# Moving the transposes of q and k to the head of a slot in an attention and GRU kernel

## The chip, the cores and the metric

The kernel runs on one core of one Trainium2 chip. The metric is the device time of one execution in microseconds (us). Before the change it is 2216.08 us, the median of 3 runs (2215.71 to 2216.1).

## The reference, cut to what matters

Two layers with residual connections work on x of shape (4, 512, 512), all in fp32. The first is attention with 16 heads of 32 columns; the second is a GRU that walks over the 512 positions one after the other.

```
# layer 0
xn  = rms_norm(x, g_norm) * (1 + scale) + shift        # scale, shift from emb @ W_emb + b_emb
q, k, v = heads(xn @ W_qkv)                            # 16 heads of 32
q, k = rms_norm(q, g_q), rms_norm(k, g_k)
attn = softmax(q @ k.T * 32 ** -0.5)
o = attn @ v
x = x + o + o @ W_out
# layer 1: GRU over 512 steps
r = sigmoid(x_t @ W_ir + h @ W_hr + b);  z = sigmoid(...)
n = tanh(x_t @ W_in + b + r * (h @ W_hn + b))
h = (1 - z) * n + z * h;   x_t = x_t + h
```

## The kernel before, in words

Each engine (TensorE is called PE, VectorE DVE, ScalarE ACT, GpSimd POOL) has its own program, written out by hand, and runs it strictly in its order; semaphores tie the programs together. The attention takes the first 556 us or so, the GRU the rest.

Attention is cut into units of one group of four heads by 128 positions. There are 4 batches x 4 groups x 4 blocks of 128 = 64 units, and every engine walks over `N_SLOTS` = 71 slots. One slot of PE works on several units at different stages (lines 395 to 474): it projects unit `n = slot` to q, k and v (`project`, line 403), transposes the normalised q and k of unit `i = slot - 2` (`transpose_qk`, line 361), forms the scores of unit `m = slot - 6`, transposes that unit's softmax weights (line 464), multiplies the transposed weights of unit `m - 1` with v (line 443), and transposes the reciprocal row sums of `m - 1` (`transpose_rexp`, line 398). In this document the last is the "rexp transpose", and the product with v is "the values". A slot's order on PE is: rexp transpose, four score matmuls (one head each, on four row groups of the array; an fp32 matmul is two instructions in the trace), the two transposes of q and k, values (on four column groups), first projection quarter, transposes of the probabilities of heads 0 and 1, second quarter, those of heads 2 and 3, third and fourth quarter.

At the end of a slot there may be a piece (`piece_of`, lines 147 to 157, and `run_piece`, line 378): four transposes of raw x ("x" piece), four transposes of scaled x ("xn" piece), or a block of eight matmuls of the output projection ("y" piece). There are 12 of each kind in the 64 slots. Each piece writes all of PSUM bank 7, `PM`. It is evicted in the next slot: an x piece by ACT (line 602), an xn piece by DVE (line 737) where its chunk is even and by ACT (line 594) where it is odd, a y piece by DVE (line 743).

The transposes of q and k write the same bank. So `transpose_qk` waits for three things (lines 361 to 370): that ACT has evicted the previous unit's q and k (`qkT_ready`), that the piece of the slot before has been evicted (`await_piece`), and that DVE has written the normalised q and k (`qn_done`, line 753). In slots 0 to 5 it is called at the end of the slot (line 471); that call is not part of the change. From slot 6 on, for units 4 to 63, it is called from line 432.

The softmax runs beside it: DVE takes the maximum of each head's scores (line 774), ACT exponentiates (line 648), PE transposes the result, DVE (line 778, heads 0 and 1) and ACT (line 653, heads 2 and 3) evict it. ACT's order in a slot is: v and the squares of the unit projected before (lines 616, 619), the eviction of an x or odd xn piece, the reciprocals (line 641), q and k (line 632), four exponentials, two evictions. DVE's is: sum of squares (line 759), the eviction of a y or even xn piece, four maxima, two evictions, reciprocal, normalised q and k, the copy that feeds the rexp transpose (line 788).

Of the kernel before, what the change touches and what calls it, by code (L numbers as in the profile page):

```python
# [46 lines left out]
LAG = 6  # L47
ALL_TILES = B * N_TILES
# [13 lines left out]
def attention_gru_kernel(nc, x, cond, W_emb, b_emb, g_norm, W_qkv, g_q, g_k, W_out,  # L62
                         W_ih, W_hh, b_ih, b_hh, out):
    with ExitStack() as ctx:
# [82 lines left out]
        def piece_of(slot):  # L147
            b, u = divmod(slot, N_TILES)
            if not 0 <= slot < ALL_TILES:
                return None  # L150
            if b >= 1 and X_SLOT <= u < X_SLOT + KT:
                return "x", b, u - X_SLOT
            if b >= 1 and Y_SLOT <= u < Y_SLOT + KT:
                return "y", b - 1, u - Y_SLOT
            if b < B - 1 and XN_SLOT <= u < XN_SLOT + KT:
                return "xn", b + 1, u - XN_SLOT
            return None
# [160 lines left out]
        def _(pe):  # L318
            def transpose(dst, src):
                return nc.tensor.transpose(dst, src, ident[:])  # L320
# [27 lines left out]
            def await_piece(slot):  # L348
                piece = piece_of(slot)
                if piece is not None:  # L350
                    kind, b, c = piece
                    if kind == "x":
                        pe.wait_ge(s["xT_ready"], b * KT + c + 1)
                    elif kind == "y":
                        pe.wait_ge(s["x1_ready"], b * KT + c + 1)
                    elif c % 2 == 0:
                        pe.wait_ge(s["xnT_dve"], 2 * b + c // 2 + 1)
                    else:
                        pe.wait_ge(s["xnT_act"], 2 * b + c // 2 + 1)

            def transpose_qk(i):
                if i == 0:
                    pe.wait_ge(s["xT_ready"], KT)
                else:
                    pe.wait_ge(s["qkT_ready"], i)
                await_piece(i + 1)
                pe.wait_ge(s["qn_done"], i + 1)
                for a in range(2):
                    last = transpose(ps[:, PM, P * a:P * a + P], qn[:, i % 2, P * a:P * a + P])
                last.then_inc(s["tqk_done"], 1)  # L370
# [7 lines left out]
            def run_piece(slot):  # L378
                kind, b, c = piece_of(slot)
                pe.wait_ge(s["qkT_ready"], slot - 1)  # L380
                if kind == "x":
                    for t in range(TT):
                        last = transpose(ps[:, PM, P * t:P * t + P], xb[:, t, P * c:P * c + P])
                    last.then_inc(s["x_ps"], 1)
                elif kind == "xn":
                    pe.wait_ge(s["xr_ready"], b * TT + TT)
                    for t in range(TT):
                        last = transpose(ps[:, PM, P * t:P * t + P], xr[:, t, P * c:P * c + P])
                    last.then_inc(s["xn_ps"], 1)
                else:  # L390
                    pe.wait_ge(ld_wout, 16)
                    pe.wait_ge(s["oT_ready"], b * G + G + 1)
                    out_projection(c, PM)

            for slot in range(N_SLOTS):
                n, i, m = slot, slot - 2, slot - LAG

                def transpose_rexp():

                    pe.wait_ge(s["rexp_done"], m)  # L400
                    transpose(ps[:, PJ[slot % 2], 3 * P:4 * P], rexp[:]).then_inc(s["rtr_done"], 1)

                def project(k):
                    b, tile = divmod(n, N_TILES)
                    g, t = divmod(tile, TT)
                    return nc.tensor.matmul(ps[:, pj(n), 0:3 * P], xnT[:, b % 2, k, P * t:P * t + P],  # L406
                                            wqkv[:, k, :].rearrange("p (a g n) -> p a g n", a=3, g=G)[:, :, g, :],
                                            start=(k == 0), stop=(k == KT - 1))

                if 0 <= m - 1 and (i < ALL_TILES or m == ALL_QUADS):  # L410
                    transpose_rexp()
                if 0 <= m < ALL_QUADS:

                    g, q = divmod(m, TT)
                    if q == 0:
                        pe.wait_ge(s["qkT_ready"], TT * g + TT)
                    for hh in range(4):

                        if m == 0:
                            pass  # L420
                        elif hh < 2:
                            pe.wait_ge(s["ptev_dve"], 2 * m - 1 + hh)
                        else:
                            pe.wait_ge(s["ptev_act"], 2 * m - 3 + hh)

                        head = slice(DH * hh, DH * hh + DH)
                        nc.tensor.matmul(ps[:, SC[hh], :], qkT[head, g % 2, 0, P * q:P * q + P], qkT[head, g % 2, 1, :],  # L427
                                         start=True, stop=True, tile_position=(DH * hh, 0)).then_inc(s["s_done"], 1)
                        if hh == 0 and i >= ALL_TILES:
                            transpose_rexp()  # L430

                if slot >= LAG and i < ALL_TILES:
                    transpose_qk(i)
                if 0 <= m - 1 < ALL_QUADS:

                    g, q = divmod(m - 1, TT)
                    if q == 0:
                        pe.wait_ge(s["oT_ready"], g + 1)
                    pe.wait_ge(s["ptev_dve"], 2 * m)
                    pe.wait_ge(s["ptev_act"], 2 * m)  # L440
                    for kc in range(TT):
                        for hh in range(4):
                            last = nc.tensor.matmul(  # L443
                                ps[QD * hh:QD * hh + QD, PO, P * q:P * q + P],
                                v_sb[:, g % G, kc, QD * hh:QD * hh + QD], probsT[:, hh, kc, :],
                                start=(kc == 0), stop=(kc == TT - 1), tile_position=(0, QD * hh))
                    last.then_inc(s["pv_done"], 1)

                if n < ALL_TILES:
                    if n % N_TILES == 0:  # L450
                        pe.wait_ge(s["xnT_dve"], 2 * (n // N_TILES) + 2)
                        pe.wait_ge(s["xnT_act"], 2 * (n // N_TILES) + 2)
                    if n >= 6:
                        pe.wait_ge(s["qn_done"], n - 1)
                    elif n >= 4:
                        pe.wait_ge(s["xT_ready"], KT)
                    if 0 <= m - 1:
                        pe.wait_ge(s["r_ready"], m)
                    project(0)
                for hh in range(4):  # L460
                    if 0 <= m < ALL_QUADS:
                        pe.wait_ge(s["exp_done"], 4 * m + hh + 1)
                        for kc in range(TT):
                            last = transpose(ps[:, SC[hh], P * kc:P * kc + P], probs[:, hh, P * kc:P * kc + P])
                        last.then_inc(s["pt_done"], 1)
                    if n < ALL_TILES and hh == 1:
                        project(1)
                if n < ALL_TILES:
                    project(2)
                    project(3).then_inc(s["proj_done"], 1)  # L470
                if slot < LAG and 0 <= i:
                    transpose_qk(i)
                if piece_of(slot) is not None:
                    run_piece(slot)
# [56 lines left out]
            for step in range(T):  # L531
# [14 lines left out]
                if n < N_BLK and q < 6 * B and step + LEAD >= 12:  # L546
                    b, i = divmod(q, 6)
# [371 lines left out]
```

## Time and profile before

| | us |
|---|---|
| median of 3 runs | 2216.08 |
| the profiled execution's own time | 2220.15 |
| its span, first to last instruction | 2218.3 |
| PE busy | 2141.1 |
| DVE busy | 1239.9 |
| ACT busy | 1150.6 |
| POOL busy | 204.8 |
| granted TensorE clock, mean | 0.999 |

The times of the table's engines are sums over the whole span. PE's matmul records overlap each other by a little, since matmuls are pipelined and their ends are modelled; the distance from one start to the next says more than a record's length. In a timeline, consecutive instructions of one kind are one row: the second number is from the first start to the last end. The number in square brackets is idle time of the engine just before the row, with what ended it; "issue" there means that the profile names no releaser. "PEld" is the loading of weights, which runs beside the matmuls.

### The profile page before, as it was taken

To read this page: it belongs to the slowest core of one execution; us is meant where nothing else is said; L and a number is where in the kernel's file an instruction comes from. 1 tells how busy PE (TensorE), PEld (TensorE's weight loads), DVE (VectorE), ACT (ScalarE), POOL (GpSimd) and SP (SyncE) were. 2 spreads that over 40 slices of the span, in tenths; PEclk is the share of its full clock that TensorE was granted. 3 is DMA by queue.
4 is the path that set the end of the run, shared out by engine and by line. 5 is a ranking of instruction groups with operands and counts; after the bars stand their busy time and mean duration, and the time that the engine had idled before them with its cause. 6 is when DMAs were issued, how large, how long until landed. Compare 5 with 4: busy or idle time off the path is not lost.

```text
span 2218.3 us, 129719 instructions
## 1 busy us (share of the span) xinstructions
PE 2141.1 (97%) x58384; PEld 1693.7 (76%) x58384; DVE 1239.9 (56%) x4460; ACT 1150.6 (52%) x4603; POOL 204.8 (9%) x235
## 2 busy tenths in 40 slices
PE   5999999999899999999999999999999999999998
PEld 3665666655688888888888888888888888888776
DVE  2665666657355555555555555555555555555554
ACT  2775665757144445454545445454545445454544
POOL 4333333322200000000000000000000000000000
PEclk9999999999999999999999999999999999999999
DMA  6000000001100001010100000010001000000000
GB/s 218 1 1 21 1 20 1 1 1 58 38 19 22 19 24 28 18 27 17 29 16 26 20 26 22 20 30 17 27 18 28 17 26 20 26 22 20 27 5 13
DMA packets 41083, 55.00 MB, mean 25 GB/s; under 512 B 9424, under 2 KB 34000, under 8 KB 40528
## 3 DMA queue, kind: packets, MB, share of 16 engines
q1 hardware_dynamic: 34112, 38.81, 5.6%
q8 instruction: 459, 7.52, 1.4%
q0 software_dynamic: 1584, 7.73, 0.9%
q10 hardware_dynamic: 4832, 0.15, 0.1%
q14 instruction: 96, 0.79, 0.1%
HBM read 29.90 MB, written 16.78 MB: 21 GB/s over the span
## 4 chain that ended last, share of the span: by engine, by line
PE 88%; DVE 5%; ACT 4%; issue 2%; ACTq 1%; POOL 1%; DMA 0%; SPq 0%; POOLq 0%; DVEq 0%
PE ps L502 58%; PE ps L320 7%; PE ps L406 7%; PE ps L488 7%; PE ps L427 3%; PE ps L443 3%; DVE znT L851 3%; PE ps L374 2%; ACT xb L689 2%; DVE xb L862 2%; ACT z_trip L686 2%; POOL qk_rs L298 0%; ACTq L575 0%; DMA seeds<-gi_spill 0%; ACTq L576 0%
## 5 line engine op out<-in xcount | busy, mean ns | idle before, releaser
L502 PE MATMUL ps<-wqkv,xb 128*4 128x128 f32 x49152 | 1472.3, 273 | 39.1 <-DVE xb L862 29.4
L502 PEld LDWEIGHTS ps<-wqkv,xb 128*4 128x4 f32 x49152 | 1219.8, 87 | 277.5 <-DVE xb L862 231.7
L686 ACT ACTIVATE z_trip<-znT 128x8 f32<-128x8 f32 x1024 | 218.3, 213 | 365.1 <-DVE znT L851 365.1
L862 DVE TENSOR_TENSOR_SCAN xb<-z_trip,xb 128x24 f32<-128x24 f32 x1024 | 213.1, 208 | 291.2 <-ACT xb L689 291.2
L867 DVE STREAM_TRANSPOSE rT<-ps 128x128 f32<-128x128 f32 x512 | 162.3, 317 | 344.3 <-PE ps L502 344.3
L851 DVE STREAM_TRANSPOSE znT<-ps 128x128 f32<-128x128 f32 x1024 | 313.0, 306 | 63.8 <-PE ps L502 2.7
L680 ACT ACTIVATE r_pair<-rT 128x16 f32<-128x16 f32 x512 | 111.6, 218 | 434.2 <-DVE rT L867 434.2
L488 PE MATMUL ps<-wih,x1T 128*32 128x256 f32 (+1 forms) x4096 | 235.7, 326 | 0.0
L689 ACT ACTIVATE xb<-v_pair 128x16 f32<-128x16 f32 x1024 | 222.7, 217 | 13.7 <-DVE v_pair L856 0.7
L856 DVE TENSOR_TENSOR_SCAN v_pair<-r_pair,znT 128x16 f32<-128x16 f32 x1024 | 196.4, 192 | 35.6 <-DVE znT L851 0.8
L406 PE MATMUL ps<-wqkv,xnT 128*128 128x384 f32 x512 | 200.5, 498 | 0.0
L664 ACT ACTIVATE ps<-seeds 128x256 f32<-128x256 f32 x512 | 188.4, 368 | 0.0
L648 ACT ACTIVATE probs<-ps,negmax 128x512 f32<-128x512 f32 x256 | 172.3, 686 | 3.2 <-DVE negmax L774 3.2
L774 DVE TENSOR_REDUCE negmax<-ps 128x1 f32<-128x512 f32 x256 | 159.3, 683 | 25.7 <-PE ps L427 25.7
L663 ACT ACTIVATE ps<-seeds 128x128 f32<-128x128 f32 x512 | 134.6, 263 | 37.5 <-DMA seeds<-gi_spill 37.5
L320 PEld LDWEIGHTS ps<-ident,probs 128*128 128x128 f32 x1024 | 118.6, 141 | 43.6 <-issue 21.3
L320 PE MATMUL ps<-ident,probs 128*128 128x128 f32 x1024 | 136.3, 274 | 1.0 <-ACT probs L648 0.7
L488 PEld LDWEIGHTS ps<-wih,x1T 128*32 128x32 f32 x4096 | 124.4, 110 | 5.9 <-issue 1.1
L298 POOL TENSOR_TENSOR qk_rs<-qk_ms,half_neg 128x8 f32<-128x8 f32 x64 | 106.6, 1666 | 11.8 <-POOL qk_ms L296 11.8
L406 PEld LDWEIGHTS ps<-wqkv,xnT 128*128 128x128 f32 x512 | 83.1, 190 | 32.0 <-issue 11.3
L759 DVE TENSOR_REDUCE qk_ss<-sq 128x8 f32<-128x256 f32 x64 | 26.9, 420 | 116.4 <-ACT sq L619 116.4
L653 ACT ACTIVATE probsT<-ps 128x512 f32<-128x512 f32 x128 | 70.1, 595 | 40.9 <-PE ps L320 40.0
(75 smaller groups left out, 981.3 us busy)
## 6 DMA issues: line engine op xcount, KB each, us to landing
gi_spill<-gi_image SPq DMA_DIRECT2D x64, 192.0 KB, 2.1
seeds<-gi_spill SPq DMA_DIRECT2D x228, 32.0 KB
seeds<-gi_spill SPq DMA_DIRECT2D x284, 16.0 KB
xb<-in_x SPq DMA_DIRECT2D x4, 1024.0 KB, 6.5
out<-xb SPq DMA_DIRECT2D x64, 64.0 KB, 2.2
wqkv<-in_L_cond_W_qkv SPq DMA_DIRECT2D x1, 3072.0 KB, 11.9
wih<-in_L_cond_W_ih POOLq DMA_DIRECT2D x1, 3072.0 KB, 14.5
wqkv<-in_L_cond_W_hh POOLq DMA_DIRECT2D x1, 3072.0 KB, 11.1
```

The costliest lines, as they stand in the source:

```text
L320: return nc.tensor.transpose(dst, src, ident[:])
L406: return nc.tensor.matmul(ps[:, pj(n), 0:3 * P], xnT[:, b % 2, k, P * t:P * t + P], wqkv[:, k, :].rearrange("p (a g n) -> p a g n", a=3, g ...
L488: last = nc.tensor.matmul(ps[QD * j:QD * j + QD, bank, first:first + width], x1T[:, k, b, BLK * block_no:BLK * block_no + BLK], gate_cols( ...
L502: last = nc.tensor.matmul(ps[QD * j:QD * j + B, bank, 0:P], hist_flat[:, first:first + 3 * B - 2:3], weights, start=False, stop=False, ski ...
L648: nc.scalar.activation(probs[:, hh, :], ps[:, SC[hh], :], ACT.Exp, bias=negmax[:, m % 2, hh:hh + 1], accum_out=sums[:, m % 2, hh:hh + 1]). ...
L664: nc.scalar.activation(ps[:, zna_bank:znb_bank + 1, 0:P].rearrange("p h (g n) -> p h g n", g=2), seeds[:, step % RING, P:3 * P].rearrange( ...
L686: nc.scalar.activation(z_trip[:, 8 * half:8 * half + 8, 2], znT[:, half, 0:16:2], ACT.Sigmoid).then_inc(s[z_name], 1)
L689: nc.scalar.activation(elements(step, half).rearrange("p (e s) -> p e s", s=3)[:, :, 0:3:2], v_pair[:, 8 * half:8 * half + 8, 1].unsqueeze ...
L851: return nc.vector.transpose(znT[:, half, :].rearrange("p (r k b s) -> p k r s b", r=4, k=4, b=B, s=2), ps[:, bank, 0:P])
L856: return nc.vector.tensor_tensor_scan(v_pair[:].rearrange("p e s -> p (e s)")[:, first:first + 16], r_pair[:].rearrange("p e s -> p (e s)" ...
L862: return nc.vector.tensor_tensor_scan(next_elements(step, half), z_trip[:].rearrange("p e s -> p (e s)")[:, 24 * half:24 * half + 24], ele ...
L867: nc.vector.transpose(rT[:], ps[:, r_bank, 0:P]).then_inc(s["rT_ready"], 1)
```

## The change: transpose_qk stands first in the slot

In the slots from 6 on, the call of `transpose_qk(i)` moves from between the scores and the values to the head of the slot, ahead of the rexp transpose and the scores. Its instructions and its three waits are the same. The programs of ACT, DVE, POOL and SP are the same.

```
+                if slot >= LAG and i < ALL_TILES:
+                    transpose_qk(i)
                 if 0 <= m - 1 and (i < ALL_TILES or m == ALL_QUADS):
                     transpose_rexp()
                 if 0 <= m < ALL_QUADS:
...
                         if hh == 0 and i >= ALL_TILES:
                             transpose_rexp()
 
-                if slot >= LAG and i < ALL_TILES:
-                    transpose_qk(i)
                 if 0 <= m - 1 < ALL_QUADS:
```

## Rows read from the trace of the kernel before

**Rows 1.** The page: the chain that ended last, by engine.
```profile
PE 88%; DVE 5%; ACT 4%; issue 2%; ACTq 1%; POOL 1%; DMA 0%; SPq 0%; POOLq 0%; DVEq 0%
```

**Rows 2.** Stretch, its length, busy us of PE, PEld, DVE, ACT, POOL; clock, DMA.
```profile
90.00:520.00 430.00, 424.92 (x3712) 268.96 (x3714) 270.04 (x565) 273.87 (x769) 150.56 (x176) 1.00 0.02 6
```

**Rows 3.** Waits of PE, 90 to 530 us: total, times, longest.
```profile
PE ps L320 <- issue: 5.1, 9, 1.5
```

**Rows 4.** Timeline of PE, a slot without a piece before it: start us, us.
```profile
130.01 0.27 PE L320 MATMUL ps<-ident,rexp 128*128 128x128 f32 x1
130.21 1.14 PE L427 MATMUL ps<-qkT 32*128 32x512 f32 x8
131.28 0.44 PE L320 MATMUL ps<-ident,qn 128*128 128x128 f32 x2
131.65 1.08 PE L443 MATMUL ps<-probsT,v_sb 128*32 128x128 f32 x32
...
133.41 1.04 PE L320 MATMUL ps<-ident,probs 128*128 128x128 f32 x8
134.29 0.81 PE L406 MATMUL ps<-wqkv,xnT 128*128 128x384 f32 x2
```

**Rows 5.** Timeline of PE, a late slot without transposes of q and k.
```profile
536.78 1.13 PE L427 MATMUL ps<-qkT 32*128 32x512 f32 x6
537.85 1.08 PE L443 MATMUL ps<-probsT,v_sb 128*32 128x128 f32 x32
```

**Rows 6.** A slot after an x piece: PE's head, ACT's eviction.
```profile
152.15 0.27 PE L320 MATMUL ps<-ident,rexp 128*128 128x128 f32 x1
...
152.35 0.60 ACT L602 ACTIVATE xT<-ps 128x512 f32<-128x512 f32 x1
```

**Rows 7.** A slot after an odd xn piece: PE's head, ACT's eviction.
```profile
100.50 0.27 PE L320 MATMUL ps<-ident,rexp 128*128 128x128 f32 x1
...
100.70 0.78 ACT L594 ACTIVATE xnT<-ps,mod_all 128x512 f32<-128x512 f32 x1
```

**Rows 8.** A slot after a y piece: PE's head, DVE's eviction.
```profile
205.87 0.27 PE L320 MATMUL ps<-ident,rexp 128*128 128x128 f32 x1
...
206.14 0.69 DVE L743 TENSOR_TENSOR x1T<-ps,xT 128x512 f32<-128x512 f32 x1 [2.50 <-PE ps L374]
```

**Rows 9.** A slot after an even xn piece, where PE waits: PE, then DVE.
```profile
92.69 0.27 PE L320 MATMUL ps<-ident,rexp 128*128 128x128 f32 x1
...
94.28 0.41 PE L320 MATMUL ps<-ident,qn 128*128 128x128 f32 x2 [0.25 <-issue]
94.62 1.08 PE L443 MATMUL ps<-probsT,v_sb 128*32 128x128 f32 x32
...
93.37 0.80 DVE L737 TENSOR_SCALAR xnT<-ps,mod_all 128x512 f32<-128x512 f32 x1
```

**Rows 10.** Slots after a batch's last y piece (first, third): PE, then DVE.
```profile
216.39 0.27 PE L320 MATMUL ps<-ident,rexp 128*128 128x128 f32 x1
...
219.20 0.41 PE L320 MATMUL ps<-ident,qn 128*128 128x128 f32 x2 [1.47 <-issue]
...
483.88 0.41 PE L320 MATMUL ps<-ident,qn 128*128 128x128 f32 x2 [0.68 <-issue]
...
218.42 0.68 DVE L743 TENSOR_TENSOR x1T<-ps,xT 128x512 f32<-128x512 f32 x1
```

**Rows 11.** Where the probabilities' weight loads wait for ACT: PE's scores, then PEld.
```profile
518.24 1.14 PE L427 MATMUL ps<-qkT 32*128 32x512 f32 x8
...
520.95 0.42 PEld L320 LDWEIGHTS ps<-ident,probs 128*128 128x128 f32 x4 [0.46 <-ACT probs L648]
521.62 0.42 PEld L320 LDWEIGHTS ps<-ident,probs 128*128 128x128 f32 x4 [0.25 <-ACT probs L648]
```

**Rows 12.** Timeline of PE at the start of the GRU, after its longest idle.
```profile
592.38 4.13 PE L502 MATMUL ps<-wqkv,xb 128*4 128x128 f32 x96 [4.29 <-ACT ps L664]
...
596.80 2.86 PE L502 MATMUL ps<-wqkv,xb 128*4 128x128 f32 x96
```

More of the change, by code:

```diff
@@ L408, in project @@
                                             start=(k == 0), stop=(k == KT - 1))
+                if slot >= LAG and i < ALL_TILES:
+                    transpose_qk(i)
                 if 0 <= m - 1 and (i < ALL_TILES or m == ALL_QUADS):
@@ L430, in _ @@
                             transpose_rexp()
-                if slot >= LAG and i < ALL_TILES:
-                    transpose_qk(i)
                 if 0 <= m - 1 < ALL_QUADS:
```

## The prediction, made before the change was built

> **What bounds the kernel now.** I read the page's chain of waits first: 88% of it is PE [rows 1]. The change touches the attention alone, so I took that stretch by itself: from 90 to 520 us PE is busy 424.92 of 430.00 us, at a granted clock of 1.00, while DVE and ACT are busy for about 270 each [rows 2]. PE is the bound, nearly without a gap; whatever idle time the new order puts on it adds to the time. The view of PE's waits says where the few gaps are: 9 waits, 5.1 us in all, each in front of a transpose, and named "issue"; by the timeline they end when the eviction of the bank does (below) [rows 3]. Then I read the timeline of one slot, to see what stands around the moved step, and last the slots that follow a piece, because the moved step waits for the eviction of bank `PM`.
>
> **The change, part by part.** I count each slot from T0, the start of its first matmul at the head, to the start of the values; what follows the values is in the same order as before. 60 calls move (units 4 to 63).
>
> *The two transposes themselves.* Before, a dense slot runs rexp 0.20 us (130.01 to 130.21), scores 1.07 (to 131.28), the transposes of q and k 0.37 (to 131.65): 1.64 in all [rows 4]. The same kind of transpose costs 0.11 where it follows another on the full array: eight of the probabilities take 0.88 (133.41 to 134.29) [rows 4]. So two cost 0.22, and the 0.15 above that is what it costs to come from the scores' row groups back to the full array. At the head they follow a projection or a piece, full array to full array. The scores then go straight over to the values, as a late slot of this trace does: scores 1.07 (536.78 to 537.85), and a record of the values that is 1.08 long, as it is behind the transposes [rows 4, 5]. New: 0.22 + 0.20 + 1.07 = 1.49, or 0.15 less in each slot; 60 x 0.15 = 9.0 us gained. Bounds: 0 gained (the switch is paid elsewhere) to 9.0; I take 9.0, since the late slot shows no such payment.
>
> The Trainium skill, "TensorEngine Tiling (Array Packing)", section Tiling Modes, says that changing the tiling mode drains TensorE. A slot had four changes (full, row groups, full, column groups, full) and has three. By that rule alone the change is a gain of the size above, and it is the third rival.
>
> *The wait for the bank.* This is the term that decides. Before, rexp and scores (1.27 us) stood between the piece and the transposes and covered its eviction. At the head nothing does; there stands only the piece's own last matmul. Restart: 94.28 is 0.11 after DVE's eviction ends (93.37 + 0.80) and 219.20 is 0.10 after (218.42 + 0.68) [rows 9, 10]. I take 0.11. Nothing that starts an eviction is moved (it waits for the piece, or for the square and its sum ahead of it), so its time from T0 stays:
> - x piece, 12 slots: eviction ends 152.35 + 0.60 = 152.95, T0 152.15; wait 0.80 + 0.11 = 0.91 [rows 6]. Net of the 0.15: +0.76 each, 9.1.
> - odd xn piece, 6 slots: 100.70 + 0.78 = 101.48, T0 100.50; wait 1.09 [rows 7]. Net +0.94, 5.6.
> - y piece, the first three of each batch, 9 slots: 206.14 + 0.69 = 206.83, T0 205.87; wait 1.07 [rows 8]. Net +0.92, 8.3.
> - even xn piece, 6 slots, and the batch's last y piece, 3 slots: these are the 9 waits of PE today. Their transposes start when the bank is free, in both orders. Before, the values follow 0.34 later (94.28 to 94.62) [rows 9]; now rexp and scores come in between: 1.49. So +1.15 each, whatever the wait is: 10.4. What had hidden the eviction in part, the scores, is now behind it.
> - 24 slots without a piece before them: -0.15 each, -3.6.
>
> Sum: 9.1 + 5.6 + 8.3 + 10.4 - 3.6 = 29.8 us. If ACT's semaphore comes when its next instruction starts, 0.1 before the record's end, 18 slots lose 0.1 less: 28. There is no slack later to give any of it back: PE has 5 us of idle in 430 [rows 2, 3], and those are used up above.
>
> *What is queued behind the wait.* The rexp transpose (then the reciprocals on ACT, needed by a projection over 2 us later) and the four scores. DVE's maxima and ACT's exponentials wait for the scores; PE wants the exponentials for its transposes of the probabilities, with 0.37 us less between scores and them than before (the two transposes stood there). Where that wait shows, the first weight loads come 520.95 - 518.24 = 2.71 us after the scores' start for head 0 and 3.38 (521.62) for head 1, then every 0.67 [rows 11]. Before, a dense slot reaches head 0 at 133.41 - 130.21 = 3.20 and head 1 at 3.64; now at 2.83 and 3.27 [rows 4]. Head 0 is in time, head 1 is 0.11 late; heads 2 and 3 come behind a projection quarter, whose record is 0.81 [rows 4], and are in time. 60 x 0.11 = 6.6. Bounds: 0 (the load gives way) and 0.11 + 0.11 (the matmul waits for its own load too, 0.42 over four [rows 11]), 13.2.
>
> *Hidden.* The two other waits, `qkT_ready` and `qn_done`, don't bind at the head: DVE writes the normalised q and k right ahead of the copy for the rexp transpose, which stands at the head today and never waits (all 9 waits are for evictions), and ACT evicted the last q and k before its four exponentials. ACT evicts q and k earlier; its first exponential waits for the first maximum anyway. No DMA and no queue of SP or POOL is passed.
>
> **Total.** 29.8 + 6.6 = 36.4. Against the profiled execution, 2220.15 + 36.4 = 2256.6; the median of the runs stands 4.07 lower, so 2252.5.
>
> **The rivals.**
> 1. *The order costs more around the scores.* The switch isn't saved (+9.0) and every slot waits 0.22 for exponentials (+6.6): 36.4 + 15.6 = 52, or 2268. For it: every ACT and DVE step of the softmax chain starts later from T0. Against: the late slot [rows 5].
> 2. *Less is lost.* The exponentials are in time (-6.6) and ACT's evictions signal early (-1.8), and the restart is shorter than 0.11 by half in 36 slots (-2.0): 26, or 2242.
> 3. *Faster.* The saved switch is 9.0 us; if the bank is free at the head, that is the result: 2216.1 - 9.0 = 2207. It decides from the point where the mean wait in the 36 slots is below 9.0 / 36 = 0.25 us. Against it: every eviction starts 0.20 us or more after T0 and takes 0.60 to 0.80.
> 4. *The clock.* The waits are idle time of PE. After 4.29 us of it the first GRU step took 4.13 us against 2.86, +1.27 [rows 12]. The longest wait will be the batch's last y piece's, 219.20 - 216.39 = 2.81 us at the head, twice, and 2.02 in the third batch, whose idle is 0.79 shorter [rows 10]; if each is followed by a slow stretch, 3 x 1.27 = +3.8, and 2256; if all 36 waits are, 36 x 1.27 = 46, and 2298. Against: the clock held at 1.00 through 1.47 us of idle [rows 2, 10].
> 5. *It doesn't do what it says*: the waits are already covered by something that I don't see, and nothing moves, 2216.
>
> **How the numbers follow.** A difference under 0.2% (4.4 us) can't be told from no change. Forecast 65%, its own range 2244 to 2262; rival 1 14%; rival 2 11%; rival 3 3%; rival 4 5%; rival 5 2%. The predicted time is 2252.5. The range 2238 to 2270 takes in rivals 1 and 2 and leaves out 3, 5 and the heavier part of 4. Slower 95%, same 2%, faster 3%.
>
> **What would show it.** In the changed trace each of the 36 slots after a piece has PE idle in front of the transposes of q and k: 0.9 to 1.1 us in 27, 1.6 in 6, 2.8 in 2 and 2.0 in 1, some 44 us in all. Dense slots have the values start 1.49 us after T0. The transposes of the probabilities wait about 0.1 us, at head 1. The GRU part is as long as before. I am wrong if PE's idle time at the head is well under 30 us, if the values start at 1.64 in dense slots, or if the clock leaves 1.00 in the attention.

## The result: 45.7 us slower, and where the time went

The changed kernel takes 2261.83 us (median of 4 runs, 2257.01 to 2264.24), the kernel before 2216.09 us beside it. The ratio is 1.0203, 95% interval 1.0185 to 1.0221. The forecast was 2252.5, its range 2238 to 2270.

The view of PE's waits shows the cause in one row (total us, times, longest). Where 9 waits summed to 5.1 us [rows 3], 36 now sum to 38.2, one for each slot that follows a piece.

```profile
PE ps L320 <- issue: 38.2, 36, 2.6
```

The timeline of PE in the changed kernel, a slot without a piece before it, answers to [rows 4]:

```profile
130.21 0.38 PE L320 MATMUL ps<-ident,qn 128*128 128x128 f32 x2
130.42 0.27 PE L320 MATMUL ps<-ident,rexp 128*128 128x128 f32 x1
130.63 1.14 PE L429 MATMUL ps<-qkT 32*128 32x512 f32 x8
131.70 1.08 PE L443 MATMUL ps<-probsT,v_sb 128*32 128x128 f32 x32
...
133.46 1.21 PE L320 MATMUL ps<-ident,probs 128*128 128x128 f32 x8
134.51 0.81 PE L406 MATMUL ps<-wqkv,xnT 128*128 128x384 f32 x2
...
137.32 0.38 PE L320 MATMUL ps<-ident,qn 128*128 128x128 f32 x2
```

The values start 131.70 - 130.21 = 1.49 us after the slot's head; it was 1.64. That is what the prediction called the saved switch of the array between row groups and full width. The eight transposes of probabilities then take 134.51 - 133.46 = 1.05, where they took 0.88 [rows 4]. That is the wait for the exponentials, 0.17. The slot is 7.11 us long, 0.02 more than before: the two cancel.

And a slot after an x piece, first PE, then ACT, which answer to [rows 6]:

```profile
151.55 0.60 PE L320 MATMUL ps<-ident,xb 128*128 128x128 f32 x4
152.89 0.41 PE L320 MATMUL ps<-ident,qn 128*128 128x128 f32 x2 [0.74 <-issue]
153.13 0.27 PE L320 MATMUL ps<-ident,rexp 128*128 128x128 f32 x1
153.34 1.14 PE L429 MATMUL ps<-qkT 32*128 32x512 f32 x8
```
```profile
152.19 0.60 ACT L602 ACTIVATE xT<-ps 128x512 f32<-128x512 f32 x1
```

The head would be at 151.55 + 0.44 (four transposes) = 151.99. ACT's eviction ends at 152.79 and the transposes start at 152.89: 0.90 us late. The bracket says 0.74, since idle time is counted from the modelled end of the last matmul, about 0.17 after the next one could start. With this 0.17 added to the idle shown, the waits are 0.91 us after an x piece, 1.09 after an odd xn piece, 1.07 after a y piece, 1.59 after an even xn piece, and 2.82, 2.82 and 2.02 after the last y piece of a batch. The 36 waits sum to 38.2 + 36 x 0.17 = 44.3 us of start-to-start time; the same sum by the predicted waits is also 44.3. Of it, the 9 old waits had already been paid in part, and the saved switch comes off.

The profiled executions differ by 2259.8 - 2218.3 = 41.5 us of span. By landmarks of their timelines: the rexp transposes of slot 7 and slot 64 are 461.25 us apart before (56.78 to 518.03) and 503.52 after (59.20 to 562.72), so 57 slots cost 42.3 more. Slot 6, the first with scores, costs 2.1 more. From slot 64 to the first GRU step nothing changes (74.35 and 74.31). The rest, the GRU, was 3.2 us shorter in the execution profiled after, with the same program; before's profiled execution (2220.15) was 4 us above its own median, so this is a difference between executions. Attention alone is 42.3 + 2.1 + 0.3 at the start = 44.7 us slower (of the 0.3, 0.1 lies ahead of slot 6, and 0.2 is there because the rexp transpose of slot 7 now stands behind the two transposes), and 2216.1 + 44.7 = 2260.8, 1 us from the median.

### The profile page after: what moved, and what is told of

Read it like the earlier page. It is cut to its first block, busy times and chain, and to the rows that moved or that the text cites. A ratio compares the mean times of both kernels' runs of the same rounds, so it can differ in the third digit from the quotient of the medians.

```text
span 2259.8 us, 129719 instructions
## 1 busy us (share of the span) xinstructions
PE 2148.3 (95%) x58384; PEld 1689.8 (75%) x58384; DVE 1234.8 (55%) x4460; ACT 1151.1 (51%) x4603; POOL 205.2 (9%) x235
## 4 chain that ended last, share of the span: by engine, by line
PE 87%; DVE 5%; ACT 4%; issue 3%; ACTq 1%; POOL 1%; DMA 0%; SPq 0%; POOLq 0%; DVEq 0%
PE ps L502 56%; PE ps L320 8%; PE ps L406 7%; PE ps L488 7%; PE ps L429 3%; PE ps L443 3%; DVE znT L851 2%; PE ps L374 2%; ACT xb L689 2%; DVE xb L862 2%; ACT z_trip L686 2%; POOL qk_rs L298 0%; ACTq L575 0%; DMA seeds<-gi_spill 0%; ACTq L576 0%
## 5 line engine op out<-in xcount | busy, mean ns | idle before, releaser
L320 PE MATMUL ps<-ident,probs 128*128 128x128 f32 x1024 | 146.1, 277 | 1.1 <-ACT probs L648 0.9
L443 PEld LDWEIGHTS ps<-probsT,v_sb 128*32 128x32 f32 x2048 | 52.2, 110 | 49.2 <-issue 49.2
```

## Experiments

Each is the kernel before with the edit that is named, and code is shown against it. The kernel before was timed again beside each of them; on other chips its median was between 2221.79 and 2228.39 us, so each time is given with its own "before", and the trace is read from the rexp transpose of slot 7 to that of slot 64, called the span of 57 slots (before: 461.25 us).

### Only the slots without a piece

```
+                at_head = slot >= LAG and i < ALL_TILES and slot > LAG and piece_of(slot - 1) is None
+                if at_head:
+                    transpose_qk(i)
...
-                if slot >= LAG and i < ALL_TILES:
+                if slot >= LAG and i < ALL_TILES and not at_head:
                     transpose_qk(i)
```

> The transposes of q and k stand at the head only in the 23 slots (from slot 7 on) that follow a slot without a piece; everywhere else they stay between scores and values. Theory A (the loss is the uncovered eviction of the bank): there is no eviction to wait for here, the saved switch of 0.15 us and the later exponentials (0.17 in the changed trace) cancel to +0.02 per slot, so +0.5 us, 2216 to 2217. Rival B (the loss is spread over all slots, through the softmax chain that starts later): 42 us / 60 x 23 = +16, 2232. Rival C (the saved switch wins where nothing is awaited): -0.15 x 23 = -3.5, 2213.

Measured: 2223.65 against 2222.58 us, ratio 1.0005 (0.9996 to 1.0015). The span of 57 slots is 461.66 (56.64 to 518.30), +0.4. Its wait row is the old one, and its dense slot has the changed kernel's shape:

```profile
PE ps L320 <- issue: 5.1, 9, 1.5
```
```profile
129.76 0.38 PE L320 MATMUL ps<-ident,qn 128*128 128x128 f32 x2
129.98 0.27 PE L320 MATMUL ps<-ident,rexp 128*128 128x128 f32 x1
130.18 1.14 PE L430 MATMUL ps<-qkT 32*128 32x512 f32 x8
131.25 1.08 PE L446 MATMUL ps<-probsT,v_sb 128*32 128x128 f32 x32
```

So the head order by itself, where nothing is awaited, costs nothing and gains nothing. The spread-out loss (B) and the gain (C) are both out.

### Only the slots after a piece

The same edit, with `at_head = slot >= LAG and i < ALL_TILES and piece_of(slot - 1) is not None`.

> The transposes stand at the head only in the 36 slots that follow a piece. Theory A: nearly the whole loss is here, 12 x 0.95 + 24 others between 0.8 and 1.7 by the changed trace, together about 40.5 us, so 2256 to 2257, with PE idle about 38 us in 36 waits. Rival B (spread over all slots): 42 / 60 x 36 = +25, 2241.

Measured: 2266.65 against 2222.58, ratio 1.0192 (1.0177 to 1.0207), and 36 waits of 38.2 us again. The span of 57 slots is 504.50 (56.16 to 560.66), +43.2: the whole loss. Of these, 2.8 us are two stretches at half clock (below; the slot in which each lies takes 10.57 us, where its like in the changed kernel takes 9.16 at full clock), so 40.4 for the waits, where 40.5 was expected.

### Only slot 6

The same edit, with `slot == LAG` as the condition.

> Only the call of slot 6 (the first with scores) is moved to the head. In the changed trace PE stands idle 2.38 us there and the clock is at half for some microseconds behind it. Theory A (the head waits for DVE's normalised q and k, which in this slot come late, and the scores are behind the wait): +2.1 us by the two traces, 2218. Rival D (that stretch was slow by the chance of the clock's phase, not by the wait): 0, 2216.

Measured: 2224.37 against 2222.58, ratio 1.0006 (0.9996 to 1.0015): the times alone don't tell +2 from 0. The timeline of PE does:

```profile
47.18 0.38 PE L320 MATMUL ps<-ident,qn 128*128 128x128 f32 x2
49.93 0.66 PE L320 MATMUL ps<-ident,qn 128*128 128x128 f32 x2 [2.37 <-DVE qn L756]
50.52 2.09 PE L430 MATMUL ps<-qkT 32*128 32x512 f32 x8
```

The scores start 50.52 - 47.18 = 3.3 us after the last transposes of the fill; before, it was 1.08 (48.51 to 49.59). They then take 2.0 us and not 1.07. The granted clock from 50.0 to 56.7 us is 0.52 (this row: stretch, length, busy us of PE, PEld, DVE, ACT, POOL, clock, DMA):

```profile
50.00:56.70 6.70, 6.70 (x22) 3.45 (x23) 3.69 (x6) 3.17 (x9) 1.99 (x2) 0.52 0.00 0
```

In this trace the slot costs 3.6 us (47.18 to the next rexp at 59.00 is 11.82; before, 48.51 to 56.78 is 8.27), in the changed kernel's 2.1. Theory A holds by the trace: PE waits for `qn` in both. What the clock adds to it varies. Rival D, that the slow stretch came by chance, isn't borne out either: all three kernels with this wait (this one, the changed one, and the one with the transposes behind the rexp transpose, below) have a slow stretch here, and the kernel before, without the wait, has none. After the 57 slots (461.25 us, as before) nothing is left of it.

### The other way: behind the values

```
                     last.then_inc(s["pv_done"], 1)
+                if slot >= LAG and i < ALL_TILES:
+                    transpose_qk(i)
...
-                if slot >= LAG and i < ALL_TILES:
-                    evacuate_qk(i)
                 if 0 <= m < ALL_QUADS:
                     for hh in range(4):
...
+                    if i < ALL_TILES:
+                        evacuate_qk(i)
```

> The transposes go the other way: behind the values, ahead of the first projection quarter, in all 60 slots; ACT evicts them behind its four exponentials, not ahead of them. Theory A: the array goes from row groups to column groups to full, three switches in place of four, -0.15 x 60 = -9.0; the scores keep their place, so the exponentials have 3.05 us to the first transposes of probabilities against 2.71 needed, no wait; the evictions are covered by 1.07 us more, so of the 9 waits (5.2 us in all) 6 vanish and 3 shrink to 0.4, 0.4 and 0, -4.4. Together -13.4, 2202 to 2204. Rival B (the switch is paid wherever the transposes stand): -4.4, 2212. Rival E (ACT's later eviction of q and k delays its evictions of the probabilities and the next scores): 2216 or above.

Measured: 2205.72 against 2222.58, ratio 0.9925 (0.9911 to 0.9940). This is faster than both kernels of the case. The span of 57 slots is 448.24 (55.46 to 503.70), -13.0. A dense slot, on PE:

```profile
126.64 0.27 PE L320 MATMUL ps<-ident,rexp 128*128 128x128 f32 x1
126.84 1.14 PE L427 MATMUL ps<-qkT 32*128 32x512 f32 x8
127.92 1.08 PE L441 MATMUL ps<-probsT,v_sb 128*32 128x128 f32 x32
128.93 0.44 PE L320 MATMUL ps<-ident,qn 128*128 128x128 f32 x2
129.20 0.81 PE L406 MATMUL ps<-wqkv,xnT 128*128 128x384 f32 x2
129.85 1.04 PE L320 MATMUL ps<-ident,probs 128*128 128x128 f32 x8
...
133.54 0.27 PE L320 MATMUL ps<-ident,rexp 128*128 128x128 f32 x1
```

It is 6.90 us long against 7.09, a saving of 0.19 and not 0.15. The eight transposes of probabilities take 0.87 (129.85 to 130.72), so nothing waits for exponentials in such a slot. The saving is 11.1 us over 57 slots (0.19 to 0.20 each), where the expectation had 9.0 over 60. The waits were overrated: 4.4 us of gain was expected from the nine slots that had one, and 2.3 came. Each of the nine is 0.45 us shorter, 0.25 more than a dense slot. For the six after an even xn piece that is the whole wait. In the three after a batch's last y piece DVE evicts late and its maxima are late too: 0.45 us of waiting for the bank is left in two of them, and 0.30 moves to the probabilities behind it (215.24 and 344.08). Slots 8 and 9 gain nothing (7.11 and 7.10 us): ACT has one more instruction ahead of its exponentials there (line 584, 0.63 us), and the eight transposes take 1.09. The misses nearly cancel (11.1 + 2.3 - 0.4 = 13.0 against 13.4), which is luck.

### Whose gain is it: ACT's order alone, and PE's alone

`act_only` makes only the ACT part of the edit above.

> The kernel before with one edit: ACT evicts the transposed q and k behind its four exponentials, not ahead of them; the transposes stay between scores and values. It tells whose gain after_values' 17 us are. Theory A (the place of the transposes on PE is what counts; the first exponential waits for the first maximum, not for this eviction): 0, 2216 to 2217. Rival F (the earlier exponentials were held up by this eviction and gave most of the gain): 5 us or more faster, below 2212.

Measured: 2221.21 against 2221.79, ratio 1.0003 (0.9994 to 1.0013), span of 57 slots 461.29. ACT's part alone gives nothing.

`values_old_act` makes only the PE part; ACT evicts q and k ahead of its exponentials, as before.

> The transposes behind the values as in after_values, but ACT's order left as before, so that its four exponentials stand behind an eviction which now waits for the transposes at scores + 2.4 us. Theory G (what is queued behind a moved wait decides): the first exponential starts about 2.8 us after the scores' start and not 1.9, head 0's weight loads are 0.65 us late, head 1's a further 0.2; 0.85 x 60 = 51 us over after_values, 2255 to 2260, slower than before by 40. Rival (ACT has slack enough): 2205 as after_values.

Measured: 2262.92 against 2221.79, ratio 1.0188 (1.0171 to 1.0205). The span of 57 slots is 499.64 (56.60 to 556.24), 51.4 over `after_values`, where 51 was expected. A dense slot is 7.84 us, 0.94 over `after_values` and not 0.85; the slots after a last y piece, where `after_values` already waited, differ by less (8.77 against 8.58), and 57 slots were measured where the estimate had 60. So the sum agrees better than its parts. PE, ACT and the weight loads:

```profile
129.12 1.14 PE L427 MATMUL ps<-qkT 32*128 32x512 f32 x8
130.20 1.08 PE L441 MATMUL ps<-probsT,v_sb 128*32 128x128 f32 x32
131.21 0.44 PE L320 MATMUL ps<-ident,qn 128*128 128x128 f32 x2
...
132.79 1.32 PE L320 MATMUL ps<-ident,probs 128*128 128x128 f32 x8 [0.50 <-ACT probs L648]
```
```profile
131.68 0.39 ACT L632 ACTIVATE qkT<-ps 128x256 f32<-128x256 f32 x1 [1.84 <-PE ps L320]
131.96 0.68 ACT L648 ACTIVATE probs<-ps,negmax 128x512 f32<-128x512 f32 x1
```
```profile
132.78 0.42 PEld L320 LDWEIGHTS ps<-ident,probs 128*128 128x128 f32 x4 [1.11 <-ACT probs L648]
```

ACT stands 1.84 us before the eviction of q and k, the first exponential starts 2.84 after the scores (129.12 to 131.96), and PE waits. The same two instructions on PE are worth -13 us or +38, by what ACT has queued behind the eviction.

### Behind the rexp transpose

This one is the changed kernel with one edit: the call stands after `transpose_rexp()`, ahead of the scores.

> The transposes stand behind the rexp transpose, still ahead of the scores. Theory A: the only thing gained over the changed kernel is that the rexp transpose (0.11 us) now covers a part of the eviction, in 36 slots: -0.11 x 36 = -4 against the changed kernel, so 37 to 42 us over before, 2254 to 2258; the 36 waits of PE sum to about 34 us and not 38. Rival H (the rexp transpose behind the wait is what costs, since ACT evicts its result ahead of q and k): most of the 42 us is gone, 2225 or less.

Measured: 2266.17 against 2221.79, ratio 1.0201 (1.0185 to 1.0216), 44.4 us, where 37 to 42 was expected. The waits came out as A has them:

```profile
PE ps L320 <- issue: 34.3, 36, 2.5
```

That is 3.9 us less than at the head. The span of 57 slots is 501.08, only 2.4 less than the changed kernel's, but the clock differs between the two. Here both waits of 2.53 us are followed by a stretch at half clock (stretch, length, busy us of PE, PEld, DVE, ACT, POOL, clock, DMA):

```profile
233.00:236.00 3.00, 3.00 (x40) 1.38 (x32) 1.69 (x3) 0.96 (x3) 2.58 (x3) 0.50 0.02 5
380.00:383.00 3.00, 3.00 (x38) 1.90 (x35) 2.48 (x4) 1.89 (x5) 2.00 (x3) 0.50 0.01 3
```

The slots behind those waits take 11.68 us each. The same slot of the third batch takes 9.05, with a wait 0.79 shorter and without the four transposes (0.44) at its end. By that the two would take about 10.3 at full clock, so each stretch costs 1.4. The changed kernel has one such stretch, of 1.3 us. Without them the spans are 498.3 and 502.2, and the difference is the 3.9 us of the wait row. The median times don't show it clearly (44.4 us over before here, 45.7 there), since a GRU that varies between executions lies over it (1631.8 us in this profiled one, 1622.8 in the changed kernel's). H is out, since nearly nothing came back.

### In the middle of the slot

The call stands at `hh == 1`, behind the transposes of heads 0 and 1, ahead of `project(1)`; ACT's order as in `after_values`.

> The transposes of q and k stand in the middle of the slot, behind the transposed probabilities of heads 0 and 1, and ACT evicts them behind its exponentials. Every eviction of the bank is covered, and between scores and probabilities there is as little work as in the changed kernel. It sets the wait for the exponentials apart from the wait for the bank. Theory A: no wait for the bank (the 9 waits go, -4.4 to -5.2 us); the switch saved, -0.15; the exponentials 0.17 late at head 1, as in the changed trace; dense slots 7.11 us, in all 3 to 5 us faster than before. Rival J (the 0.17 belongs to the head order, by the softmax chain starting later in the slot): dense slots 6.90 to 6.94, and 14 to 17 us faster, as after_values.

Measured: 2225.49 against 2228.39, ratio 0.9991 (0.9981 to 1.0000); span of 57 slots 460.65 (56.52 to 517.17), -0.6. PE, dense slot:

```profile
130.07 1.14 PE L427 MATMUL ps<-qkT 32*128 32x512 f32 x8
131.14 1.08 PE L441 MATMUL ps<-probsT,v_sb 128*32 128x128 f32 x32
...
132.90 1.21 PE L320 MATMUL ps<-ident,probs 128*128 128x128 f32 x8
133.95 0.38 PE L320 MATMUL ps<-ident,qn 128*128 128x128 f32 x2
```

No wait for the bank is left, and the eight transposes still take 1.05 (132.90 to 133.95). The 0.17 is there with 2.83 us between scores and probabilities (130.07 to 132.90), whether or not the slot begins with a wait. J is out. The gain in the span, 0.6 us, is smaller than the 3 to 5 expected; the medians are 2.9 us apart, and the interval of their ratio reaches 1. The six slots after an even xn piece did gain their wait (7.58 us against 7.81). In the three after a batch's last y piece DVE does the late eviction and then the maxima, so that there most of the wait only moves to the exponentials: the first of them takes 8.81 us against 9.03, and PE's waits read

```profile
PE ps L320 <- ACT probs L646: 2.9, 5, 1.0
```

Three of the five waits in this row are in these slots (0.98, 0.97 and 0.18). The 0.02 by which every other slot is longer takes another 1.0 back, and slots 8 and 9 take 7.32 us, another 0.4.

### Behind the first projection quarter

The call stands after `project(0)`; ACT's order as in `after_values`.

> The transposes stand behind the first projection quarter, one step later than in after_values; ACT evicts them behind its exponentials. Theory A: same number of switches, same work between scores and probabilities (2.83 + 0.22 = 3.05 us against 2.71 needed), and 0.7 us more cover, so that the last two waits for the bank (0.9 us in after_values) go: equal to after_values to within 1 us, 14 to 18 us faster than before. Rival (the saving in after_values came from filling the way back from the column groups, which the first quarter now pays with 0.75 instead of 0.64): dense slots 0.1 longer, 8 to 11 us faster than before.

Measured: 2216.70 against 2228.39, ratio 0.9945 (0.9930 to 0.9960), 11.7 us; span of 57 slots 450.32 (55.29 to 505.61), -10.9; dense slots 6.94. It lies between the two expectations. The saving of a dense slot is 0.15 here and 0.19 behind the values, so 0.04 x 57 = 2.3 of the 13.0 us there came from the place of the transposes right behind the values. Transposes and first quarter take 0.92 us in that order (128.93 to 129.85) and 0.97 in this one (129.03 to 130.00). The last 0.9 us of waits for the bank went, as expected, but brought next to nothing: the waits for exponentials rose from 0.8 to 1.7 us, and the slot after the first batch's last y piece takes 8.59 us here and 8.58 there.

## Why the prediction was right, step by step

**The bound.** PE without slack: held. In `piece_only` the waits come back in the span to 0.1 us (40.4 of 40.5).

**The switch, -0.15 per slot.** Measured 1.49 us from head to values in dense slots, as worked out. That a switch is saved and not shifted, `dense_only` can't show, since the wait for exponentials takes the gain away. `after_values` and `after_first` show it: nothing waits for exponentials in their dense slots, and these are 0.19 and 0.15 us shorter. The Trainium skill's rule of the drain (TensorEngine Tiling (Array Packing), Tiling Modes) agrees with the sign in both. What in the switch costs the time is not settled. The weight loads of the transposes are seen in the traces to change with the order. Before, behind row groups, they start with the matmul at 131.28 [rows 4]; in the changed kernel, behind the full array, the first starts 0.33 us ahead of the matmul at 130.21:

```profile
131.28 0.20 PEld L320 LDWEIGHTS ps<-ident,qn 128*128 128x128 f32 x2 [0.76 <-issue]
```
```profile
129.88 0.14 PEld L320 LDWEIGHTS ps<-ident,qn 128*128 128x128 f32 x1
```

A load of 0.14 us that is no longer hidden would be about the price of 0.15. That is an estimate from these rows; no run sets it apart from a drain.

**The wait for the bank, +29.8 net of the switch.** This was the right mechanism at the right size. The starts of the transposes fit in each of the five kinds, as the predicted sum of 44.3 us does. `piece_only` has the whole loss and `dense_only` none of it.

**The exponentials, +6.6.** Right mechanism, mis-sized: 0.17 us per slot and not 0.11, +3.6 in all. The weight loads came as worked out (scores at 130.63, loads at +2.71 and +3.38):

```profile
133.34 0.47 PEld L320 LDWEIGHTS ps<-ident,probs 128*128 128x128 f32 x4 [0.34 <-ACT probs L648]
134.01 0.42 PEld L320 LDWEIGHTS ps<-ident,probs 128*128 128x128 f32 x4 [0.20 <-ACT probs L648]
```

What the prediction left out of its value, though not of its bounds, is what follows the late load: head 1's first matmul starts with it, at 134.01, and the second comes 0.17 us later (134.18) and not 0.11. That is the other 0.06. `mid_slot` shows the same 0.17 without the head order.

**"The two other waits don't bind at the head."** This failed in one slot. The argument took a steady slot; in slot 6 the pipeline is still filling, DVE's normalised q and k come late, and nothing stood between the fill and this wait but the scores that were moved behind it. `slot6_only` shows the wait; it is 2.1 us in the changed kernel's trace.

**The clock.** The prediction held the clock at 1.00 and named a clock that leaves it as a sign of being wrong. It left it twice: in slot 6, and once behind a long wait, which is rival 4 (5%) in a third of its small form. PE's timeline around the longest head wait of the second batch, and the clock behind it:

```profile
380.07 0.66 PE L320 MATMUL ps<-ident,qn 128*128 128x128 f32 x2 [2.65 <-issue]
380.53 0.42 PE L320 MATMUL ps<-ident,rexp 128*128 128x128 f32 x1
380.88 2.09 PE L429 MATMUL ps<-qkT 32*128 32x512 f32 x8
```
```profile
381.00:384.00 3.00, 3.00 (x40) 1.34 (x40) 1.01 (x2) 0.82 (x3) 2.50 (x3) 0.62 0.04 8
```

This slot and the rest of its wait cost 1.3 us more than their like one batch earlier (10.26 + 13.59 us between rexp transposes against 9.16 + 13.39).

**The sum.** 36.4 + 3.6 (exponentials) + 2.1 (slot 6) + 1.3 (clock) = 43.4; the remaining 1.3 of 44.7 is 0.02 us per slot from rounding in the rows and 0.3 at the start. The three misses have one sign, which is why the time came out 9.3 us above the forecast, at the upper end of the forecast's own range of 2244 to 2262 and well inside the stated one. Slot 6 and the clock are costs of a wait that the sum put at nothing; the exponentials were a term in it that was too small.

## What to carry to other kernels

Before an instruction with several waits is moved up, list what stood between the signal and the wait, since that was its cover, and look in a steady slot, in the slots with extra work and in the first slot. Moving it down can be worth more: here it kept the saved switch and lengthened the cover, and was 0.75% faster than before instead of 2.0% slower. But the engine that consumes the result must be reordered with it; the same move without that cost 1.9%.

## What the runs showed of the hardware

- The granted clock fell to half (1.2 of 2.4 GHz) behind most idle times of PE of 2.4 us and more, and not behind all. In the changed kernel, one of two waits of 2.65 us was followed by a slow stretch (0.62 over 3 us); in `piece_only`, both of 2.64 (0.50 over 232 to 235 us, 0.51 over 378.5 to 381.5), and with the transposes behind the rexp transpose, both of 2.53 (0.50), each for some 1.4 us of time. After the 34 shorter waits (at most 1.85 us) no slot of the first two traces was longer than its like. Slot 6, after 2.4 us, ran at 0.62 (51.7 to 56.2 us) in the changed kernel and 0.52 in `slot6_only`.
- Two transposes cost 0.22 us after full-array work, 0.37 after row groups, and 0.27 after column groups, where the projection quarter behind them then takes 0.64 and not 0.75. Behind the column groups, transposes and quarter took 0.92 us with the transposes first and 0.97 with the quarter first.
- The GRU, the same program in all kernels, took 1622.8 to 1638.3 us in the profiled executions. Changes of a few microseconds in attention were readable from landmarks of the timeline and not from single times.
